# One block turn and two transfers in place of eight score transposes, in a four-layer graph network

## The chip, the cores and the metric

The kernel runs on one core of one Trainium2 chip. The core has five engines: TensorE (PE, matrix products), VectorE (DVE), ScalarE (ACT), GpSimd (POOL) and SyncE (SP), which here only issues transfers (DMA). Each engine works through its own instructions in order, and they meet through semaphores. The metric is the time of one execution in microseconds; less is better.

## The reference

A batch of 32 graphs with 256 nodes and 128 features passes through four graph layers, each with a residual and a layer norm:

```python
x = _layernorm(x + L0(x, adj, adj, ...))   # gated neighbour sums
x = _layernorm(x + L1(x, adj, ...))        # two linear layers with batch norms over all nodes
x = _layernorm(x + L2(x, adj, W, a))       # attention
x = _layernorm(x + L3(x, adj, ...))        # two graph convolutions, then LSTMs over windows of 1 to 4 nodes
```

The change is in the attention, and around it:

```python
Wh = jnp.einsum('bnf,fo->bno', h, W)
s1, s2 = Wh @ a1, Wh @ a2
e = s1[:, :, None] + s2[:, None, :]
e = jnp.where(e >= 0, e, 0.2 * e)
e = jnp.where(adj[None] == 0, -jnp.inf, e)
h_prime = jnp.einsum('bij,bjo->bio', jax.nn.softmax(e, axis=-1), Wh)
```

So each node i has a score s1[i], and the row of all s2[j] of its graph must stand beside it: the second score has to be spread from one value per partition (a node is a partition) to a row of 256 values that every partition holds.

## The kernel before, in words

The batch is cut into 8 groups of 4 graphs; a group is 8 tiles of 128 nodes x 128 features (two tiles a graph). The layers L0 and L1 come first for all groups, since the batch norms need every node. Then the groups go through attention (A), the graph convolutions of L3 (B), the LSTMs (L) and the last norm (T) in a pipeline of slots: slot s = 2 to 9 holds A of group s, B of group s - 1, L of group s - 2 and T of group s - 3, as far as these groups exist. Groups 0 and 1 have their attention ahead of the slots. A is in the slots 2 to 7, T from slot 3 on; slot 8 has B, L and T, slot 9 has only L and T and cuts its LSTM into two lanes so that one computes while the other waits. The order of every engine's work in a slot is written out by hand in one function `slot` per engine (L491 for SyncE, L631 GpSimd, L1026 TensorE, L1372 ScalarE, L1974 VectorE), so what stands behind what is read there.

The LSTMs are eleven steps k = 0 to 10 (windows of 1, 1, 2, 2, 3, 3, 3, 4, 4, 4, 4 nodes). A step is: x(k), TensorE's product of the inputs (L958); h(k), its product of the last state (L984), for all but the first step of a window; the gates on ScalarE (L1334); the cell on VectorE (`lstm_cell`, L1846; the first step of a window needs only this line); the tanh of the cell on ScalarE (L1370); the state on VectorE (`lstm_state`, L1874). In the code `inner(k)` is the cell, `state(k)` the state, `cell(k)` both. h(k) waits for the state of step k - 1, and so does the x(k) that begins the windows of another length: x(4) waits for state 3, x(7) for state 6. Where a step is done in halves, L1892 to L1904 and L1871 stand for the cell and the first half of the state.

Around the change in a slot with A:

- VectorE: statistics of the first norm (L1721, L1549 to L1559); `t_blocks` (L1945), which turns 32 x 32 blocks of a finished LSTM group for its way back to node order; the cell and state of step 2; `a_dots` (L1728), sixteen products-and-sums of the residual tiles with two vectors, which give both scores before scaling; `a_s12` (L1734), scores times rstd; the cell and state of step 3; `a_max` (L1745), eight times: row of scores plus mask, and its maximum; the cell and state of step 4.
- GpSimd: rstd of the first norm (L526), OFF = mean x rstd (L532), then `scaled(s + 2)` (L586), the batch norm's scale on a group that comes two slots later, which returns at once for s = 6 and 7; later the copies of `carry_residual` (L604) and `carry_blocks` (L614), which wait for turns by VectorE.
- ScalarE: gates and tanh of step 2, `a_spread` (L1304), eight `norm_apply` (L1169), the gates of step 3.
- TensorE: x(3), h(3), `a_rows` (L854), `a_weigh0` (L923), x(4), x(5), h(5), x(6), `a_weigh1` (L932), h(6), `a_spread1` (L941), x(7), x(8) and so on. `a_rows` takes column t of S12, repeated 128 times, and transposes it with the identity: that gives one 128-column piece of the row of scores, on all partitions, in PSUM (PA).
- SyncE: `weave` (L484) stores the turned blocks to DRAM, waits for the store, and loads them back in another order in four transfers; `t_sum` (L1952) on VectorE waits for those. Behind it in the queue stand `move_residual`, `move_blocks` and the store of the output.

Slot 8 ends B: `a_hidden` (L1834) on VectorE takes the relu of `a_spread1`'s whole result into HT, the LSTM's input. In slot 9 `t_blocks` stands between step 0 and step 1; the products of lane 1 for step 2 (L1006, PA) wait for state 1.

Of the kernel before, what the change touches and what calls it, by code (L numbers as in the profile page):

```python
# [20 lines left out]
F32 = mybir.dt.float32  # L21
# [79 lines left out]
def build(nc, x, xt, adj, early_in, later_in, lstm_w, out):  # L101
    ctx = ExitStack()
    with ctx:
# [164 lines left out]
        def before(g):  # L268
# [25 lines left out]
        ln = [{s: sem(f"ln{k}_{s}") for s in ("stats", "sum", "dif", "sqd", "mean", "m2", "var", "rstd", "off", "out")} for k in range(4)]  # L294
# [4 lines left out]
        (yt_ok, y_ps, z1_ok, x2t_ps, x2t_ok, s2_ps, wh_ps, wh_ok, max_ok, eb_a, eb_ok, lin_ok, exps_ok,  # L299
         et_ps, pt_ok, att_ps, rd_ok, z2_ok, sp_ps, sp_ok, y0_ps, y0_ok, h0_ok, y1_ps,  # L300
         y1_ok, h1_ps, h1_ok, ht_ok, zf_ok) = (sem(n) for n in (
             "yt_ok", "y_ps", "z1_ok", "x2t_ps", "x2t_ok", "s2_ps", "wh_ps", "wh_ok", "max_ok", "eb_a",
# [114 lines left out]
        BLOCKS = late[:, 2, COLS:2 * COLS]  # L417

# [25 lines left out]
        def _(sp):  # L444
# [219 lines left out]
        def _(pe):  # L664
# [165 lines left out]
            def a_scores(g, h):  # L830
                pe.wait_ge(x2t_ok, halves(g, h))
                f = front(g)
                pe.matmul(f.PB[:, h * BANK:(h + 1) * BANK], WA2[:], f.X2T[:, h * BANK:(h + 1) * BANK],
                          start=True, stop=True).then_inc(s2_ps, 1)
# [191 lines left out]
            def slot(s, par, A, B, L, T):  # L1026
# [55 lines left out]
                a_rows(s) if A else None  # L1082
# [79 lines left out]
        def _(act):  # L1162
# [115 lines left out]
            def a_lin(g, some):  # L1278
                f = front(g)
                for b in some:  # L1280
                    act.wait_ge(wh_ok, 2 * g + b // 2 + 1) if g < 2 else act.wait_ge(s12_ok, g - 1)
# [90 lines left out]
            def slot(s, par, A, B, L, T):  # L1372
# [104 lines left out]
        def _(dve):  # L1477
# [245 lines left out]
            def a_dots(g):  # L1723
                dve.wait_ge(z1_ok, 2 * (g - 1))
                dve.wait_ge(rows_ok, 1)
                for k, junk in enumerate((one_a, one_c)):
                    for t in range(TILES):
                        dve.tensor_tensor_reduce(nth(junk, t), nth(Z, t), WAR[:, k], 1.0, 0.0,  # L1728
                                                 ALU.mult, ALU.add, DOT[:, k, t:t + 1]).then_inc(dots_ok, 1)

            def a_s12(g):
                dve.wait_ge(dots_ok, 2 * TILES * (g - 1))
                dve.wait_ge(ln[1]["rstd"], 2 * (g + 1))
                dve.tensor_tensor(S12[:], DOT[:], RSD[0][:].unsqueeze(1).broadcast_to([P, 2, TILES]), ALU.mult).then_inc(s12_ok, 1)  # L1734

            def a_max(g, h=None):

                dve.wait_ge(s2_ps, halves(g, h))
# [8 lines left out]

            def a_bias(g, h=None):

                ts = tls(h)  # L1750
                dve.wait_ge(wh_ok, halves(g, h)) if g < 2 else dve.wait_ge(s12_ok, g - 1)
# [190 lines left out]
            def t_blocks(g, par):  # L1942
                dve.wait_ge(h_ok, NSTEP * (g + 1))
                for c in range(NC):
# [29 lines left out]
            def slot(s, par, A, B, L, T):  # L1974
# [65 lines left out]
                a_hidden(s - 1, 1 - par) if B and not A else None  # L2040
# [114 lines left out]
```

## Time and profile before

| | |
|---|---|
| median of 3 runs | 616.72 us (616.62 to 617.77) |
| the profiled execution | 617.1 us, span of its instructions 615.3 us |
| TensorE busy | 596.5 us, 97% of the span, 2560 products |
| VectorE busy | 495.3 us, 80% |
| ScalarE busy | 431.7 us, 70% |
| GpSimd busy | 242.3 us, 39% |
| granted TensorE clock | 0.997 of full speed, mean over the span |
| chain that ended last | TensorE 62%, VectorE 10%, ScalarE 8% of the span |

A timeline row gives the start and the length of a group of instructions in us, its engine, its source line (L854 is line 854), the operation, the tiles (out<-in), shapes, and in brackets how long the engine stood idle before it and which instruction ended that. Instructions of one engine overlap a little, so the time that one costs is the distance to the next start. TensorE's products are pipelined and their ends are modelled: one row may seem to reach some 0.17 us into the next. The groups of the page merge all instructions of one line and shape.

### The profile page before, as it was taken

What the parts mean: (1) busy time and instruction counts of PE and PEld (TensorE: products, weight loads), DVE (VectorE), ACT (ScalarE), POOL (GpSimd) and SP (SyncE); (2) the same over time, 40 slices, a digit from 0 to 9 for tenths busy, and PEclk for the clock granted to TensorE, in tenths of its full rate; (3) what the DMA queues carried; (4) which work ended last, traced back from release to release, by engine and by line L of the source; (5) the groups of instructions that cost most, each with busy time, mean ns of one, the idle gap of its engine ahead of it and who ended that gap; (6) DMA issues with size and microseconds to landing.
All of it is one profiled execution on the core that took longest, in us unless ns stands there. A gap on an engine that the chain in (4) does not pass through costs nothing.

```text
span 615.3 us, 9582 instructions
## 1 busy us (share of the span) xinstructions
PE 596.5 (97%) x2560; PEld 416.8 (68%) x2560; DVE 495.3 (80%) x1673; ACT 431.7 (70%) x1000; POOL 242.3 (39%) x384
## 2 busy tenths in 40 slices
PE   8999999999999999999999999999999999999994
PEld 6645556447886687678658767865876686675894
DVE  3999999876857778889888988888898878466576
ACT  3678877965947776785778668567867867556774
POOL 1465461005134074238607733860673075003013
PEclk9999999999999999999999999999999999999998
DMA  8434000000000010201111110111112011100201
GB/s 320 158 137 172 0 3 0 0 1 1 2 2 1 0 42 3 69 14 40 60 35 36 44 68 10 35 63 42 31 47 70 1 35 69 35 0 34 70 2 69
DMA packets 14982, 28.00 MB, mean 46 GB/s; under 512 B 2896, under 2 KB 10192, under 8 KB 14800
## 3 DMA queue, kind: packets, MB, share of 16 engines
q1 hardware_dynamic: 14928, 27.40, 12.9%
q8 instruction: 20, 0.33, 0.2%
q14 instruction: 34, 0.28, 0.1%
HBM read 15.72 MB, written 7.86 MB: 38 GB/s over the span
## 4 chain that ended last, share of the span: by engine, by line
PE 62%; DVE 10%; ACT 8%; issue 4%; POOL 1%; DVEq 0%; POOLq 0%; ACTq 0%
PE QQ L958 19%; PE QQ L984 13%; PE PA L941 4%; PE PB L932 2%; ACT X L1169 2%; PE PA L914 2%; PE PB L792 2%; PE PA L792 2%; PE PB L894 2%; PE PA L894 2%; DVE HB L1745 1%; ACT raw L1334 1%; PE QQ L973 1%; PE QQ L1006 1%; PE PA L745 1%
## 5 line engine op out<-in xcount | busy, mean ns | idle before, releaser
L1334 ACT ACTIVATE raw<-QQ,BL 128x256 f32<-128x256 f32 (+2 forms) x279 | 149.3, 558 | 67.1 <-PE QQ L984 29.4
L958 PE MATMUL QQ<-HT,WT 128*128 128x512 f32 (+2 forms) x516 | 163.7, 464 | 0.1
L958 PEld LDWEIGHTS QQ<-HT,WT 128*128 128x128 f32 x516 | 96.1, 190 | 53.3 <-issue 26.8
L526 POOL TENSOR_TENSOR RSD<-VAR,pw 128x4 f32<-128x4 f32 (+1 forms) x43 | 59.4, 1381 | 153.9 <-DVE VAR L1559 153.9
L984 PE MATMUL QQ<-HB,WT 128*128 128x256 f32 (+2 forms) x336 | 100.8, 443 | 1.6 <-DVE HB L1874 1.4
L984 PEld LDWEIGHTS QQ<-HB,WT 128*128 128x128 f32 x336 | 61.1, 190 | 32.6 <-issue 13.4
L604 POOL COPY HB<-HB 32x256 f32<-32x256 f32 x60 | 27.4, 456 | 96.5 <-DVE HB L1696 93.1
L1370 ACT ACTIVATE raw<-raw 128x256 f32<-128x256 f32 (+4 forms) x79 | 37.2, 471 | 29.7 <-DVE raw L1856 19.8
L614 POOL COPY HB<-HB 32x256 f32<-32x256 f32 x96 | 40.8, 425 | 33.0 <-DVE HB L1767 26.9
L1846 DVE SCALAR_TENSOR_TENSOR raw<-raw 128x256 f32<-128x256 f32 (+2 forms) x60 | 32.1, 535 | 9.6 <-ACT raw L1334 8.7
L594 POOL TENSOR_SCALAR X<-four,MEAN,RSD 128x128 f32<-128x128 f32 x64 | 37.4, 596 | 1.6
L1169 ACT ACTIVATE X<-Z,OFF,RSD 128x128 f32<-128x128 f32 x80 | 31.8, 482 | 2.5 <-POOL OFF L532 2.5
L1874 DVE SCALAR_TENSOR_TENSOR HB<-raw 128x256 f32<-128x256 f32 (+4 forms) x42 | 22.0, 525 | 13.5 <-ACT raw L1370 13.5
L1297 ACT ACTIVATE HB<-HB,EB 128x256 f32<-128x256 f32 x64 | 30.8, 499 | 0.2
L745 PE MATMUL PA<-AHT,X 128*128 128x256 f32 x128 | 29.6, 384 | 1.3 <-ACT X L1169 1.3
L628 POOL TENSOR_SCALAR four<-HB,MEAN,RSD 128x128 f32<-128x128 f32 x56 | 30.0, 549 | 0.7
L914 PE MATMUL PA<-AD,X 128*128 128x256 f32 x128 | 30.2, 379 | 0.0
L759 PE MATMUL QQ<-one_b,later 128*128 128x512 f32 x64 | 29.1, 597 | 0.6 <-ACT one_b L1203 0.6
L941 PE MATMUL PA<-AD,Y 128*128 128x256 f32 x128 | 29.2, 380 | 0.0
L914 PEld LDWEIGHTS PA<-AD,X 128*128 128x128 f32 x128 | 24.2, 190 | 7.1 <-issue 4.1
L745 PEld LDWEIGHTS PA<-AHT,X 128*128 128x128 f32 x128 | 23.7, 190 | 7.7 <-issue 4.8
L941 PEld LDWEIGHTS PA<-AD,Y 128*128 128x128 f32 x128 | 24.2, 190 | 4.3
(260 smaller groups left out, 1213.9 us busy)
## 6 DMA issues: line engine op xcount, KB each, us to landing
four<-in_x SPq DMA_DIRECT2D x8, 512.0 KB, 4.1
raw<-in_xt SPq DMA_DIRECT2D x8, 512.0 KB, 7.1
HB<-HB SPq DMA_DIRECT2D x116, 32.0 KB, 1.8
woven<-HB SPq DMA_DIRECT2D x7, 512.0 KB, 2.6
HB<-woven SPq DMA_DIRECT2D x28, 128.0 KB, 2.8
out<-four SPq DMA_DIRECT2D x7, 512.0 KB, 2.7
WT<-in_lstm SPq DMA_DIRECT2D x1, 2048.0 KB, 8.0
later<-in_later SPq DMA_DIRECT2D x1, 725.5 KB, 10.5
```

Of the source, the lines that this page charges most:

```text
L526: pool.tensor_tensor(RSD[kk][:, ts], VAR[kk][:, ts], pw[:, ts], ALU.pow).then_inc(ln[k]["rstd"], some)
L594: pool.tensor_scalar(tile_of(X1, g, c, b), nth(f.Z2, t), MEAN[f.kk2][:, t:t + 1], RSD[f.kk2][:, t:t + 1], ALU.add, ALU.mult).then_inc(ln[2 ...
L614: pool.tensor_copy(block_at(1, h, c, q), block_at(0, h, q, c)).then_inc(carried_ok, 1)
L745: mm = pe.matmul(PA[:, b * NODES:(b + 1) * NODES], tile_of(X1, g, m, b), AHT[:, m, :], start=(m == 0), stop=(m == NC - 1))
L914: mm = pe.matmul(PA[:, b * NODES:(b + 1) * NODES], tile_of(X1, g, m, b), ADJT[:, m, :], start=(m == 0), stop=(m == NC - 1))
L941: mm = pe.matmul(PA[:, b * NODES:(b + 1) * NODES], turned(Y, m, b), ADJT[:, m, :], start=(m == 0), stop=(m == NC - 1))
L958: mm = pe.matmul(steps_view(Q[q], k), WT[:, 0, (p - 1) * 4 + q, :], ht_view(par, k), start=True, stop=(s == 0))
L984: pe.matmul(Q[q][:, 0:nw * GB], WT[:, 1, (p - 1) * 4 + q, :], HS[:, (k - 1) % 2, 0:nw * GB], start=False, stop=True).then_inc(g_ps, 1)
L1169: act.activation(nth(to, t), nth(z, t), ACT.Identity, bias=OFF[kk][:, t:t + 1], scale=RSD[kk][:, t:t + 1]).then_inc(ln[k]["out"], 1)
L1334: act.activation(TG[q][:, at:n], Q[q][:, at:n], ACT.Tanh, scale=0.5 if q == G else 0.25, bias=BL[:, p - 1, q:q + 1]).then_inc(g_ok, 1)
L1370: act.activation(TC[:, at:n], CELL[:, at:n], ACT.Tanh, scale=0.5).then_inc(tc_ok, 1)
L1846: dve.scalar_tensor_tensor(out=target[:, 0:n], in0=TG[I][:, 0:n], scalar=1.0, in1=TG[G][:, 0:n], op0=ALU.add, op1=ALU.mult).then_inc(cell_ ...
```

## The change

In the slots 2 to 7 `a_rows` goes. VectorE makes the second score first: its eight dots, then times rstd (`a_score(s, 1)`), then `a_turn_scores`, one 32 x 32 block turn of the eight scores each repeated 32 times, which leaves each 32-partition block with its own 256 scores in a row. SyncE stores one row of each block to DRAM (`scores`, 4 KB), waits for it, and loads all 1024 scores to every partition (`ROWS`, 512 KB), at the head of the slot's queue. `a_max` becomes `a_max_some` and reads ROWS in SBUF instead of PA in PSUM; six of its tiles stand ahead of the cell of step 4 and two behind it. The dots of the first score stand between and behind the cell and the state of step 2, and `t_blocks` behind them. A part of `t_sum` moves from ahead of state 4 to behind the cell and the state of step 5. `a_spread1` no longer waits for the maxima.

In slot 8 `a_spread1` is cut in two halves, behind x(8) and behind x(9), and the relu of `a_hidden` goes from VectorE to ScalarE, also in halves. In slot 9 `t_blocks` goes from behind step 0 to behind step 1, its second half behind the first cell of lane 1.

```diff
@@ SyncE
+            def spread_scores(g):
+                sp.wait_ge(s2_ok, halves(g, None))
+                sp.wait_ge(ln[2]["out"], TILES * 2) if g == 2 else None
+                sp.dma_start(scores[g].rearrange("(t q i) -> q t i", q=4, i=32),
+                             BYROW[0:P:32].rearrange("q (t i) -> q t i", i=32)).then_inc(scores_in, 16)
+                sp.wait_ge(scores_in, 32 * (g - 2) + 16)
+                sp.dma_start(ROWS, scores[g].unsqueeze(0).broadcast_to([P, TILES * P])).then_inc(scores_in, 16)
             for s in range(2, GROUPS + 2):
+                spread_scores(s) if s < GROUPS else None
                 weave(s - 3) if s >= 3 else None
@@ TensorE
-            def a_rows(g):
-                pe.wait_ge(s12_ok, g - 1)
-                reach(pe, sp_ok, 2 * g)
-                for b in range(GB):
-                    for c in range(NC):
-                        t = 2 * b + c
-                        mm = pe.transpose(turned(PA, c, b), S12[:, 1, t:t + 1].broadcast_to([P, P]), ident[:])
-                mm.then_inc(s2_ps, 2)
...
-                pe.wait_ge(max_ok, upto(g + 2) * TILES) if g else None
...
-                    a_spread1(LAST)
-                    for k in range(7, NSTEP):
-                        x(k)
-                        h(k) if STEPS[k][1] else None
+                    x(7)
+                    x(8)
+                    a_spread1(LAST, 0)
+                    h(8)
+                    x(9)
+                    a_spread1(LAST, 1)
+                    h(9)
+                    x(10)
+                    h(10)
...
-                a_rows(s) if A else None
@@ ScalarE
-                a_mixed(s, (0, 1)) if A else None
+                a_mixed(s, (0, 1)) if A else a_hidden(LAST, 1 - par, 0) if B else None
                 gates(9)
                 state(9)
-                a_mixed(s, (2, 3)) if A else None
+                a_mixed(s, (2, 3)) if A else a_hidden(LAST, 1 - par, 1) if B else None
@@ VectorE
+            def a_score(g, k):
+                dve.wait_ge(dots_ok, 2 * TILES * (g - 2) + (2 - k) * TILES)
+                dve.wait_ge(ln[1]["rstd"], 2 * (g + 1))
+                dve.tensor_tensor(S12[:, k], DOT[:, k], RSD[0][:], ALU.mult).then_inc(s12_ok, 1)
+            def a_turn_scores(g):
+                dve.wait_ge(s12_ok, 2 * (g - 2) + 1)
+                dve.transpose(BYROW.rearrange("p (t i) -> p t i", i=32),
+                              S12[:, 1].unsqueeze(2).broadcast_to([P, TILES, 32])).then_inc(s2_ok, 2)
+            def a_max_some(g, a, b):
+                dve.wait_ge(scores_in, 32 * (g - 1))
+                for t in range(a, b):
+                    dve.tensor_tensor_reduce(MS[:, t], ROWS[:, t // 2 * NODES:(t // 2 + 1) * NODES], NEG[:, t % 2], 1.0, -3e38,
+                                             ALU.add, ALU.max, MX[0][:, t:t + 1]).then_inc(max_ok, 1)
...
                 if s == LAST + 2:
                     cell(0)
-                    t_blocks(s - 3, 1 - par)
                     cell(1)
+                    t_blocks(s - 3, 1 - par, 0)
                     for k in range(LANED, NSTEP):
                         for l in range(2):
                             lane_cell(k, l)
+                            t_blocks(s - 3, 1 - par, 1) if (k, l) == (LANED, 1) else None
...
                     norm_small(1, 0, s)
-                t_blocks(s - 3, 1 - par) if T else None
-                cell(2)
                 if A:
-                    a_dots(s)
-                    a_s12(s)
+                    a_dots(s, 1, 0, TILES)
+                    a_score(s, 1)
+                    a_turn_scores(s)
+                inner(2)
+                a_dots(s, 0, 0, 4) if A else None
+                state(2)
+                if A:
+                    a_dots(s, 0, 4, TILES)
+                    a_score(s, 0)
+                t_blocks(s - 3, 1 - par, 0, 1) if T else None
                 cell(3)
-                a_max(s) if A else None
+                a_max_some(s, 0, 6) if A else None
                 inner(4)
-                t_sum(s - 3, (0,)) if T else None
+                a_max_some(s, 6, TILES) if A else None
                 state(4)
                 a_biased0(s - 1) if B else None
                 a_bias(s) if A else None
                 t_sum(s - 3, (1,)) if T else None
                 inner(5)
-                t_sum(s - 3, (2, 3)) if T else None
+                t_sum(s - 3, (0, 2)) if T else None
                 state(5)
+                t_sum(s - 3, (3,)) if T else None
...
-                a_hidden(s - 1, 1 - par) if B and not A else None
```

## Rows read from the trace of the kernel before

**Rows 1.** TensorE's timeline, s = 5: start, us, engine, line, operation, tiles, shapes, count.

```profile
365.86 1.04 PE L854 MATMUL PA<-ident,S 128*128 128x128 f32 x8
366.73 1.88 PE L923 MATMUL PB<-one_b,later 128*128 128x512 f32 x4
368.45 4.24 PE L958 MATMUL QQ<-HT,WT 128*128 128x340 f32 x14
372.74 2.55 PE L984 MATMUL QQ<-HB,WT 128*128 128x340 f32 x8
```

**Rows 2.** VectorE's timeline, s = 5; bracketed: idle time before, its end.

```profile
356.85 2.11 DVE L1945 STREAM_TRANSPOSE HB<-HT 128x512 f32<-128x512 f32 x2
358.87 0.66 DVE L1846 SCALAR_TENSOR_TENSOR raw<-raw 128x512 f32<-128x512 f32 x1
360.29 1.01 DVE L1874 SCALAR_TENSOR_TENSOR HB<-raw 128x512 f32<-128x512 f32 x1 [0.77 <-ACT raw L1370]
...
367.95 0.42 DVE L1874 SCALAR_TENSOR_TENSOR HT<-raw 128x256 f32<-128x256 f32 x1
368.28 0.42 DVE L1745 CUSTOM_DVE_ANT_0 HB<-PA,NEG 128x256 f32<-128x256 f32 x1
...
371.04 0.51 DVE L1846 SCALAR_TENSOR_TENSOR raw<-raw 128x340 f32<-128x340 f32 x1
...
372.17 0.51 DVE L1874 SCALAR_TENSOR_TENSOR HB<-raw 128x340 f32<-128x340 f32 x1 [0.29 <-ACT raw L1370]
```

**Rows 3.** ScalarE's timeline, s = 5.

```profile
359.56 0.63 ACT L1370 ACTIVATE raw<-raw 128x512 f32<-128x512 f32 x1 [1.12 <-DVE raw L1846]
...
364.08 1.24 ACT L1334 ACTIVATE raw<-QQ,BL 128x512 f32<-128x512 f32 x2
```

**Rows 4.** VectorE's groups of instructions, whole span: busy us, mean ns, idle before.

```profile
L1728 DVE CUSTOM_DVE_ANT_0 one_c<-Z,WAR 128x128 f32<-128x128 f32 x48 | 10.6, 282 | 0.0
```

**Rows 5.** GpSimd's timeline, s = 5.

```profile
351.96 1.49 POOL L526 TENSOR_TENSOR RSD<-VAR,pw 128x4 f32<-128x4 f32 x1 [2.04 <-DVE VAR L1559]
...
357.09 1.64 POOL L526 TENSOR_TENSOR RSD<-VAR,pw 128x8 f32<-128x8 f32 x1 [1.25 <-DVE VAR L1559]
358.89 0.70 POOL L532 TENSOR_TENSOR OFF<-MEAN,RSD 128x8 f32<-128x8 f32 x1 [0.17 <-POOL RSD L526]
359.58 1.19 POOL L586 TENSOR_SCALAR HB<-HB,BN 128x1024 f32<-128x1024 f32 x1
```

**Rows 6.** GpSimd's timeline, s = 2.

```profile
195.53 0.20 POOL L532 TENSOR_TENSOR OFF<-MEAN,RSD 128x8 f32<-128x8 f32 x1 [0.17 <-POOL RSD L526]
195.71 1.20 POOL L586 TENSOR_SCALAR HB<-HB,BN 128x1024 f32<-128x1024 f32 x1
```

**Rows 7.** VectorE's timeline, s = 2.

```profile
196.00 1.44 DVE L1874 SCALAR_TENSOR_TENSOR HB<-raw 128x512 f32<-128x512 f32 x1 [0.77 <-ACT raw L1370]
```

**Rows 8.** DMA issues of the page: count, KB each, us from issue to landing.

```profile
woven<-HB SPq DMA_DIRECT2D x7, 512.0 KB, 2.6
```

**Rows 9.** TensorE's timeline, s = 8 and 9.

```profile
544.79 3.62 PE L941 MATMUL PA<-AD,Y 128*128 128x256 f32 x16
548.24 3.19 PE L958 MATMUL QQ<-HT,WT 128*128 128x256 f32 x14
552.04 1.99 PE L984 MATMUL QQ<-HB,WT 128*128 128x256 f32 x8 [0.61 <-DVE HB L1874]
...
556.27 1.99 PE L984 MATMUL QQ<-HB,WT 128*128 128x256 f32 x8 [0.51 <-DVE HB L1874]
...
570.40 0.70 PE L1006 MATMUL PA<-HT,WT 128*128 128x256 f32 x2 [1.55 <-DVE HT L1874]
```

**Rows 10.** VectorE's timeline, s = 8 and 9.

```profile
546.48 0.33 DVE L1874 SCALAR_TENSOR_TENSOR HT<-raw 128x172 f32<-128x172 f32 x1
...
568.60 0.71 DVE L1888 SCALAR_TENSOR_TENSOR raw<-raw 128x256 f32<-128x256 f32 x2
```

**Rows 11.** ScalarE's timeline, s = 9.

```profile
566.02 2.06 ACT L1334 ACTIVATE raw<-QQ,BL 128x512 f32<-128x512 f32 x3
```

More of the change, by code:

```diff
@@ L293, in build @@
         rows_ok, dots_ok, s12_ok, px_ps, px_ok = (sem(n) for n in ("rows_ok", "dots_ok", "s12_ok", "px_ps", "px_ok"))
-        ln = [{s: sem(f"ln{k}_{s}") for s in ("stats", "sum", "dif", "sqd", "mean", "m2", "var", "rstd", "off", "out")} for k in range(4)]
+        ln = [{s: sem(f"ln{k}_{s}") for s in ("stats", "sum", "dif", "sqd", "mean", "m2", "var", "rstd", "off", "out") if (k, s) != (2, "off")}
+              for k in range(4)]
+        scores_in = sem("scores_in")
         agg1_ps, agg1_ok, hid_ps, hid_ok, hid_st = (
@@ L298, in build @@
         act_ok, out2_ps, out2_ok, out2_st = (sem(n) for n in ("act_ok", "out2_ps", "out2_ok", "out2_st"))
-        (yt_ok, y_ps, z1_ok, x2t_ps, x2t_ok, s2_ps, wh_ps, wh_ok, max_ok, eb_a, eb_ok, lin_ok, exps_ok,
+        (yt_ok, y_ps, z1_ok, x2t_ps, x2t_ok, s2_ok, wh_ps, wh_ok, max_ok, eb_a, eb_ok, lin_ok, exps_ok,
          et_ps, pt_ok, att_ps, rd_ok, z2_ok, sp_ps, sp_ok, y0_ps, y0_ok, h0_ok, y1_ps,
          y1_ok, h1_ps, h1_ok, ht_ok, zf_ok) = (sem(n) for n in (
-             "yt_ok", "y_ps", "z1_ok", "x2t_ps", "x2t_ok", "s2_ps", "wh_ps", "wh_ok", "max_ok", "eb_a",
+             "yt_ok", "y_ps", "z1_ok", "x2t_ps", "x2t_ok", "s2_ok", "wh_ps", "wh_ok", "max_ok", "eb_a",
              "eb_ok", "lin_ok", "exps_ok", "et_ps", "pt_ok", "att_ps", "rd_ok", "z2_ok", "sp_ps",
@@ L417, in build @@
         BLOCKS = late[:, 2, COLS:2 * COLS]
+        scores = nc.dram_tensor("scores", (GROUPS, TILES * P), F32, kind="Internal").ap()
+        BYROW = late[:, 2, 0:NODES]
+        ROWS = four[:, 1]
         def stored(g):
@@ L833, in a_scores @@
                 pe.matmul(f.PB[:, h * BANK:(h + 1) * BANK], WA2[:], f.X2T[:, h * BANK:(h + 1) * BANK],
-                          start=True, stop=True).then_inc(s2_ps, 1)
+                          start=True, stop=True).then_inc(s2_ok, 1)
             def a_project(g, h):
@@ L1280, in a_lin @@
                 for b in some:
-                    act.wait_ge(wh_ok, 2 * g + b // 2 + 1) if g < 2 else act.wait_ge(s12_ok, g - 1)
+                    act.wait_ge(wh_ok, 2 * g + b // 2 + 1) if g < 2 else act.wait_ge(s12_ok, 2 * (g - 1))
                     act.wait_ge(max_ok, TILES * g + 2 * b + 2)
@@ L1312, in a_state, with a_hidden @@
                 act.wait_ge(h1_ps, halves(0, h))
+                act.activation(by_batch(HT[:, par])[:, 2 * h:2 * h + 2], PA[:, part(h)].rearrange("p (b n) -> p b n", n=NODES),
+                               ACT.Relu, scale=2.0).then_inc(h1_ok, 1)
+            def a_hidden(g, par, h):
+                act.wait_ge(h1_ps, halves(g, h))
+                reach(act, ht_ok, 2 * (g - 1))
                 act.activation(by_batch(HT[:, par])[:, 2 * h:2 * h + 2], PA[:, part(h)].rearrange("p (b n) -> p b n", n=NODES),
@@ L1721, in a_norm1_some, with a_dots @@
                     dve.bn_stats(STL[0][:, t, :], nth(Z, t)).then_inc(ln[1]["stats"], 1)
-            def a_dots(g):
+            def a_dots(g, k, a, b):
                 dve.wait_ge(z1_ok, 2 * (g - 1))
                 dve.wait_ge(rows_ok, 1)
[L1726 to L1732, printed above, removed]
-                dve.wait_ge(ln[1]["rstd"], 2 * (g + 1))
-                dve.tensor_tensor(S12[:], DOT[:], RSD[0][:].unsqueeze(1).broadcast_to([P, 2, TILES]), ALU.mult).then_inc(s12_ok, 1)
+                for t in range(a, b):
+                    dve.tensor_tensor_reduce(nth((one_a, one_c)[k], t), nth(Z, t), WAR[:, k], 1.0, 0.0,
+                                             ALU.mult, ALU.add, DOT[:, k, t:t + 1]).then_inc(dots_ok, 1)
+            def a_score(g, k):
+                dve.wait_ge(dots_ok, 2 * TILES * (g - 2) + (2 - k) * TILES)
+                dve.wait_ge(ln[1]["rstd"], 2 * (g + 1))
+                dve.tensor_tensor(S12[:, k], DOT[:, k], RSD[0][:], ALU.mult).then_inc(s12_ok, 1)
[3 more added lines that the diff above has]
+                              S12[:, 1].unsqueeze(2).broadcast_to([P, TILES, 32])).then_inc(s2_ok, 2)
             def a_max(g, h=None):
-                dve.wait_ge(s2_ps, halves(g, h))
+                dve.wait_ge(s2_ok, halves(g, h))
                 reach(dve, att_ps, GB * before(g))
@@ L1746, in a_max @@
                                                  ALU.add, ALU.max, f.MX[:, t:t + 1]).then_inc(max_ok, 1)
+            def a_max_some(g, a, b):
+                dve.wait_ge(scores_in, 32 * (g - 1))
+                for t in range(a, b):
+                    dve.tensor_tensor_reduce(MS[:, t], ROWS[:, t // 2 * NODES:(t // 2 + 1) * NODES], NEG[:, t % 2], 1.0, -3e38,
+                                             ALU.add, ALU.max, MX[0][:, t:t + 1]).then_inc(max_ok, 1)
             def a_bias(g, h=None):
                 ts = tls(h)
-                dve.wait_ge(wh_ok, halves(g, h)) if g < 2 else dve.wait_ge(s12_ok, g - 1)
+                dve.wait_ge(wh_ok, halves(g, h)) if g < 2 else dve.wait_ge(s12_ok, 2 * (g - 1))
                 dve.wait_ge(max_ok, TILES * g + ts.stop)
@@ L1940, in lane_state, with t_blocks @@
                                          in1=steps_view(TC, k)[:, a:b], op0=ALU.add, op1=ALU.mult).then_inc(v.h, 1)
-            def t_blocks(g, par):
+            def t_blocks(g, par, *some):
                 dve.wait_ge(h_ok, NSTEP * (g + 1))
-                for c in range(NC):
+                for c in some:
                     dve.transpose(BLOCKS.rearrange("p (r c b i) -> p c b r i", r=4, c=NC, b=GB)[:, c],
```

## The prediction

> **What bounds the kernel now.** I read the page first, then TensorE's timeline over one full slot, then the chain of waits over the same slot, and last VectorE, ScalarE and GpSimd side by side in its front half. Slot s = 5 stands for s = 2 to 7, whose rows repeat.
>
> TensorE issues back to back. In [rows 1] each group starts where the one before it ended, counted by columns: the eight transposes of `a_rows` fill 365.86 to 366.73 (0.87 us), `a_weigh0` fills 366.73 to 368.45, then come x(4) and x(5) (14 instructions), then h(5) at 372.74. So TensorE work that goes away seems to pay in full. It doesn't have to: x(4) may start only when VectorE has written the state of step 3, and that ends at 367.95 + 0.42 = 368.37 [rows 2]. The chain of waits says the same: in the front half of a slot it runs on VectorE and ScalarE, and from h(5) to the slot's end on TensorE alone. The front half is a tie, within 0.1 us at x(4) and some 0.2 us at h(5). Whatever leaves TensorE there leaves a hole unless state 3 comes earlier.
>
> What sets state 3 is one line of work. VectorE: two block turns (L1945) from 356.85, then the cell of step 2 (L1846) at 358.87 [rows 2]. ScalarE waits for that cell (1.12 us idle), takes its tanh at 359.56, then works without a pause through `a_spread` and eight `norm_apply` to the gates of step 3 at 364.08 [rows 3]; from there to state 3 it is 368.37 - 364.08 = 4.3 us. A delay of the cell of step 2 goes one to one into state 3, and x(4).
>
> **The change in the slots s = 2 to 7.** Ahead of the cell of step 2 the change takes out the block turns, 358.87 - 356.85 = 2.02 us [rows 2], and puts in eight dots, the score times rstd, and the spreading turn. Dots: 10.6 us for 48 in [rows 4], 0.22 each, so 1.77 us: 356.85 to 358.62. The score waits for GpSimd's rstd, which ends at 357.09 + 1.64 = 358.73 [rows 5]. GpSimd can be held up by a dot that it meets: the rstd at 351.96, met by a state update of VectorE, took 1.49 us for a smaller tile. I allow 0.1 us: 358.85. The small product and its hand-over to the turn are estimated at 0.25 us. The turn writes 256 columns per partition; no row shows one from a repeated column. By L1945 (2.02 us for 1024) it is 0.50 us, by the 256-column operations of L1745 ((371.04 - 368.28)/8 = 0.345 us) it is 0.35 us [rows 2]; I take 0.4, both ends stay in the range. So the cell of step 2 could start at 359.5, 0.65 us late.
>
> It then meets GpSimd. In s = 2 to 5 the queue of GpSimd goes on from rstd to OFF (L532) and to `scaled` (L586, 1.19 us on 1024 columns) [rows 5]; in s = 6 and 7 `scaled` returns at once. While L586 runs, a VectorE operation that reads two SBUF tiles stands still: in s = 2, L586 ends at 195.71 + 1.20 = 196.91 [rows 6], and L1874, begun at 196.00, took 1.44 us and ended at 197.44 [rows 7], 0.53 us after L586, whereas an operation of its size takes 0.66 (L1846 in [rows 2]). In s = 5 the same L1874 took 1.01 us beside L586 [rows 2]. In the kernel before it was the cell that came first: L532 took 0.70 us there against 0.20 in s = 2 [rows 5, 6], being held until the cell ended. After the change the order turns over: L532 starts 0.16 us after rstd, takes 0.20, so L586 starts at 359.2, before the cell is ready at 359.5, and ends at 360.4. The cell ends 0.53 us later, at 360.95, where it ended at 358.87 + 0.66 = 359.53. The shift is 1.4 us.
>
> The Trainium skill, page SBUF — State Buffer, section Who interferes with whom, has this as a rule that speaks against the change: a VectorE instruction with two SBUF inputs contends with a GpSimd instruction that reads SBUF, and the one that issues first keeps the port for its whole length. By that rule the sum for these slots is the one made here; without it, it is that of the first rival. The two L1874 agree with it.
>
> State 3 then comes at 368.37 + 1.4 = 369.8, x(4) at 369.85. Without `a_rows` TensorE is ready at 368.45 - 0.87 = 367.58 and stands idle 2.3 us. x(4) and x(5) take 372.74 - 368.45 - 0.2 = 4.1 us, so h(5) starts at 373.95: **+1.2 us a slot** for s = 2 to 5, 4.8 in all. h(5) also needs state 4. Six maxima instead of eight stand ahead of the cell of step 4, from 368.28 + 1.4 to 371.75; state 4 follows as before by 372.17 - 371.04 + 0.51 = 1.64 us, at 373.4 [rows 2]. That is earlier than TensorE needs it, so the two maxima moved behind the cell (0.69 us) gain nothing. In s = 6 and 7 only the 0.65 us counts: x(4) at 369.1, h(5) at 373.2, **+0.45 us** each, 0.9 in all.
>
> Edits at nothing, with their cover. The other eight dots, the second product and the moved block turns (1.77 + 0.25 + 2.02 us) stand on VectorE behind state 2 and end before the gates of step 3 (shifted to 365.5) reach it; if that cover were gone they would add to state 3. State 2 itself comes near 362.5 and h(3) may wait 0.1 to 0.2 us for it, which `a_weigh0` and the idle time absorb. The maxima read SBUF now instead of PSUM: the dots read two SBUF tiles and cost no more per column. GpSimd has nothing to run at that time, since `carry_residual` waits for turns made later. The sums of `t_sum` change places after h(5), where VectorE waits for ScalarE and TensorE.
>
> The transfers: SyncE's queue now holds the score's store, a wait for its landing, and a 512 KB load ahead of `weave`. Behind that wait stand `weave` and, behind it, `move_residual`. The rows land in about 2.6 us for each (the nearest row, 512 KB to `woven` [rows 8]), so ROWS stands near 366 at the latest and the maxima want it at 369.7. The weave starts after the moved block turns (near 365.7), needs two such times, some 371.5, and `t_sum` wants it after 375. Cost taken: 0, at most 2 us a slot if the load were three times slower than that row.
>
> **The last two slots.** In s = 8 `a_spread1` (16 instructions, 548.24 - 544.79 = 3.45 us [rows 9]) no longer covers the wait for state 6, which ends at 546.48 + 0.33 = 546.81 [rows 10]: x(7) starts at 546.9, 2.1 us after TensorE is free. x(7) and x(8) take 14 x 0.2156 = 3.0 us and half of `a_spread1` 1.7: h(8) at 551.6 (before: 552.04). h(8), x(9) and the other half, 24 x 0.2156 = 5.2, put h(9) at 556.8 (before: 556.27 [rows 9]). The two waits are filled, but the new one is larger: **+0.5 us** (0.2 to 0.9). The relu on ScalarE falls into its gaps; if it didn't, x(0) of the next slot would wait for it. In s = 9 TensorE waited 1.55 us at 570.40 for state 1 [rows 9], whose cell stood behind the block turns until 568.60 [rows 10]. With the turns behind state 1 the cell goes when ScalarE has the gates; the tanh can't start before ScalarE ends the third gate at 566.02 + 2.06 = 568.08 [rows 11], against about 569.0 (cell's first half from 568.60): **-1.0 us** (-0.7 to -1.55). The block turns then hide while TensorE works on both lanes.
>
> **Sum.** 4.8 + 0.9 + 0.5 - 1.0 = +5.2 us. The profiled execution took 617.1 us (span 615.3), which is 0.4 above the median 616.72: 622.3 for such an execution, 621.9 for a median.
>
> **The rivals.**
> *The cell gets past GpSimd* (the score is ready sooner than I think, or L586 doesn't hold this cell). Then all six slots cost 0.45 us: 2.7 - 0.5 = +2.2, 618.9. For it: my margin in the race is only 0.3 us. Against it: the two L1874 [rows 2, 7]. With a quick turn and 0.25 us a slot it is +1.0, which can't be told from no change. Chance 0.14 above that line and 0.09 within it.
> *GpSimd's rstd waits for all eight dots.* Each dot reads two SBUF tiles, and the rstd at 351.96 took half a microsecond more beside one such operation [rows 5]. If rstd starts at 358.65 rather than 357.09, the cell shifts by 1.5 us more in all six slots: +9, 631. Against it: there the delay ended with one operation. With transfers that come late (the same sign), chance 0.09.
> *Faster: the path ahead of the cell is shorter after all.* The place is the cell of step 2, and the point from which it decides is 358.87: if it starts no later, x(4) stays at 368.45, the moved maxima count, h(5) gains 0.2 us in six slots, and with 1.55 us in s = 9 and nothing lost in s = 8 it is -2.8, 613.9. Against it: rstd ends at 358.73 and three steps follow it. Chance 0.05.
> *The change does not relieve TensorE at all* (transposes gone, hole in their place) is part of my forecast, not beside it.
>
> **How the numbers follow.** Forecast 621.9 with chance 0.63: its own range runs from 619.5 (turn 0.35, slot 9 at its best) to 624.5 (turn 0.5, rstd held 0.2 us, 1.5 us a slot). With the first rival the range reaches down to 617.9; a little of the third up to 625.5. A measurement of this kernel can tell some 0.2%, 1.2 us, from no change. Faster 0.05, within 0.2% 0.09, slower 0.86.
>
> **What would show it.** Right: in s = 2 to 5 L1846 of step 2 takes some 1.3 us or more and ends 0.5 us after L586; x(4) starts over 1 us after `a_weigh0` has run out, with TensorE idle before it; in s = 6 and 7 that idle time is smaller by 0.7 us; TensorE is idle 2 us before x(7) of s = 8, and less than 1 us at state 1 of s = 9. Wrong: L1846 starts before L586 in these slots, or x(4) follows `a_weigh0` at once, or the maxima wait for the load of the scores.

## The result, and the profile after

The changed kernel takes 626.9 us in the median (625.4 to 628.5) beside 616.8 us: a ratio of 1.016, 95% interval 1.0144 to 1.0175. The forecast was 621.9 us (617.9 to 625.5): the sign was right, the loss twice as large. The profiled execution, the slowest of the four, took 628.5 us; its span is 626.5 us against 615.3, and its mean granted clock 0.986 against 0.997. In the new file lines move: L1846 is now L1872, L1874 is L1900, L1370 is L1386, L586 is L601, L958 is L963, L984 is L989, L923 is L929, L941 is L946; L1753 is the new turn. In the experiments' files they can lie a few lines further on.

VectorE in s = 5, where [rows 2] showed the cell of step 2 at 358.87 with 0.66 us (start us, us, engine, line, operation, tiles, shapes):

```profile
365.43 0.45 DVE L1753 STREAM_TRANSPOSE HB<-S 128x256 f32<-128x256 f32 x1
365.80 1.34 DVE L1872 SCALAR_TENSOR_TENSOR raw<-raw 128x512 f32<-128x512 f32 x1
...
375.57 0.42 DVE L1900 SCALAR_TENSOR_TENSOR HT<-raw 128x256 f32<-128x256 f32 x1
375.90 0.42 DVE L1771 CUSTOM_DVE_ANT_0 HB<-four,NEG 128x256 f32<-128x256 f32 x1
```

GpSimd and ScalarE in the same slot, against [rows 5] and [rows 3]:

```profile
363.42 1.64 POOL L541 TENSOR_TENSOR RSD<-VAR,pw 128x8 f32<-128x8 f32 x1 [1.25 <-DVE VAR L1575]
365.22 0.20 POOL L547 TENSOR_TENSOR OFF<-MEAN,RSD 128x8 f32<-128x8 f32 x1 [0.17 <-POOL RSD L541]
365.41 1.20 POOL L601 TENSOR_SCALAR HB<-HB,BN 128x1024 f32<-128x1024 f32 x1
```

```profile
367.18 0.63 ACT L1386 ACTIVATE raw<-raw 128x512 f32<-128x512 f32 x1 [2.40 <-DVE raw L1872]
```

The scale of GpSimd starts at 365.41, ahead of the cell, and ends at 366.61; the cell takes 1.34 us and ends at 367.14, 0.53 us later. In s = 7, where the scale isn't there, the same cell behind the same turn takes 0.65 us:

```profile
478.01 0.65 DVE L1872 SCALAR_TENSOR_TENSOR raw<-raw 128x512 f32<-128x512 f32 x1
```

The rest of the line follows: ScalarE idles 2.40 us where it idled 1.12, state 3 is written from 375.57 on, and the maxima (L1771) follow at once: they do not wait for the transfers (nor in the other five slots), whose issues SyncE's timeline shows at 365.90 and 367.61:

```profile
365.90 0.57 SPq L500 DMA_DIRECT2D scores<-HB  x1
367.61 0.34 SPq L503 DMA_DIRECT2D four<-scores  x1
```

TensorE, x(4) and x(5) of s = 2, 3 and 4 (206.17, 263.37, 320.55), h(5) of s = 4 (324.66), then s = 5, against [rows 1]:

```profile
206.17 5.96 PE L963 MATMUL QQ<-HT,WT 128*128 128x340 f32 x14 [1.96 <-DVE HT L1900]
...
263.37 5.96 PE L963 MATMUL QQ<-HT,WT 128*128 128x340 f32 x14 [1.97 <-DVE HT L1900]
...
320.55 4.27 PE L963 MATMUL QQ<-HT,WT 128*128 128x340 f32 x14 [1.96 <-DVE HT L1900]
324.66 2.45 PE L989 MATMUL QQ<-HB,WT 128*128 128x340 f32 x8
...
372.19 1.88 PE L929 MATMUL PB<-one_b,later 128*128 128x512 f32 x4
376.04 5.96 PE L963 MATMUL QQ<-HT,WT 128*128 128x340 f32 x14 [1.97 <-DVE HT L1900]
381.84 2.45 PE L989 MATMUL QQ<-HB,WT 128*128 128x340 f32 x8
```

One idle time, then the stretches behind those of s = 5, 4 and 8 (window in us, its length, time in which TensorE was busy with the number of its instructions, granted clock, share of the DMA engines, GB/s):

```profile
374.10:376.00 1.90, 0.00 (x0) 1.00 0.26 74
376.04:381.80 5.76, 5.76 (x14) 0.70 0.21 66
320.60:324.50 3.90, 3.90 (x14) 1.00 0.38 106
556.65:561.60 4.95, 4.95 (x15) 0.66 0.01 3
```

Here lies what the forecast left out. `a_weigh0` starts at 372.19 and, by [rows 1], fills 1.72 us; x(4) starts at 376.04, so TensorE is idle 2.13 us, as forecast (2.3). But then the same fourteen products of x(4) and x(5) take 5.80 us (376.04 to 381.84) in s = 5 and 4.11 us (320.55 to 324.66) in s = 4. In s = 5 the granted clock of that stretch is 0.70, for part of it the lower of the two levels (1.2 GHz); in s = 4 it is 1.00. That costs 1.7 us each time. Call such a fall of the clock a drop. In this execution there are four, behind the idle times of s = 2, 3, 5 and 8: four times 1.7 us, or 6.8 us.

From one h(5) to the next the kernel before needs 54.50 us, from its h(5) of s = 4 (the row stops at the end of its window; only its start is read),

```profile
318.24 1.98 PE L984 MATMUL QQ<-HB,WT 128*128 128x340 f32 x6
```

to 372.74 [rows 1]. After, s = 4 to s = 5 takes 381.84 - 324.66 = 57.18, 2.68 more; s = 3 to s = 4, without the drop, takes 55.50 (269.16 to 324.66), 0.97 more than before (263.71 to 318.24).

In s = 6 and 7 the scale isn't there and the idle time is shorter; the clock stays, and the group takes 4.27 us where it took 5.96:

```profile
432.77 4.27 PE L963 MATMUL QQ<-HT,WT 128*128 128x340 f32 x14 [1.52 <-DVE HT L1900]
...
487.56 4.27 PE L963 MATMUL QQ<-HT,WT 128*128 128x340 f32 x14 [1.27 <-DVE HT L1900]
```

The last two slots, against [rows 9]:

```profile
556.65 4.98 PE L963 MATMUL QQ<-HT,WT 128*128 128x256 f32 x14 [1.91 <-DVE HT L1900]
561.46 1.89 PE L946 MATMUL PA<-AD,Y 128*128 128x256 f32 x8
...
581.70 0.70 PE L1011 MATMUL PA<-HT,WT 128*128 128x256 f32 x2 [0.47 <-DVE HT L1900]
```

x(7) waits 1.91 us for state 6, and x(7) and x(8) take 4.81 us where 3.0 were counted, at a granted clock of 0.66. State 1 of s = 9 is waited for 0.47 us instead of 1.55.

### The profile page after: what moved, and what is told of

It is laid out like the page before. It is cut to its first block, busy times and chain, and to the rows that moved or that the text cites. A ratio compares the mean times of both kernels' runs of the same rounds, so it can differ in the third digit from the quotient of the medians.

```text
span 626.5 us, 9518 instructions
## 1 busy us (share of the span) xinstructions
PE 597.4 (95%) x2512; PEld 416.0 (66%) x2512; DVE 498.4 (80%) x1684; ACT 432.5 (69%) x1002; POOL 241.0 (38%) x384
## 4 chain that ended last, share of the span: by engine, by line
PE 60%; ACT 10%; DVE 9%; issue 4%; POOL 2%; DVEq 0%; ACTq 0%; POOLq 0%
PE QQ L963 23%; PE QQ L989 11%; PE PA L946 4%; ACT X L1178 3%; PE PB L938 2%; ACT raw L1350 2%; PE PB L807 2%; PE PA L807 2%; POOL RSD L541 2%; PE PB L900 2%; PE PA L900 2%; PE PA L760 1%; DVE HT L1900 1%; PE PA L920 1%; DVE raw L1872 1%
## 5 line engine op out<-in xcount | busy, mean ns | idle before, releaser
L963 PE MATMUL QQ<-HT,WT 128*128 128x512 f32 (+2 forms) x516 | 170.7, 480 | 12.7 <-DVE HT L1900 12.6
L963 PEld LDWEIGHTS QQ<-HT,WT 128*128 128x128 f32 x516 | 99.7, 197 | 70.3 <-issue 30.9
L989 PE MATMUL QQ<-HB,WT 128*128 128x256 f32 (+2 forms) x336 | 100.0, 440 | 0.6 <-DVE HB L1900 0.6
L989 PEld LDWEIGHTS QQ<-HB,WT 128*128 128x128 f32 x336 | 61.5, 190 | 29.4 <-issue 11.2
L1386 ACT ACTIVATE raw<-raw 128x256 f32<-128x256 f32 (+4 forms) x79 | 37.1, 470 | 34.0 <-DVE raw L1882 20.1
L1872 DVE SCALAR_TENSOR_TENSOR raw<-raw 128x256 f32<-128x256 f32 (+2 forms) x60 | 34.4, 574 | 13.7 <-ACT raw L1350 13.1
L946 PE MATMUL PA<-AD,Y 128*128 128x256 f32 x128 | 29.4, 380 | 0.0
L946 PEld LDWEIGHTS PA<-AD,Y 128*128 128x128 f32 x128 | 24.3, 191 | 4.2
L1900 DVE SCALAR_TENSOR_TENSOR HB<-raw 128x256 f32<-128x256 f32 (+4 forms) x42 | 20.3, 483 | 8.0 <-ACT raw L1386 8.0
```

The costliest lines, as they stand in the source:

```text
L963: mm = pe.matmul(steps_view(Q[q], k), WT[:, 0, (p - 1) * 4 + q, :], ht_view(par, k), start=True, stop=(s == 0))
L989: pe.matmul(Q[q][:, 0:nw * GB], WT[:, 1, (p - 1) * 4 + q, :], HS[:, (k - 1) % 2, 0:nw * GB], start=False, stop=True).then_inc(g_ps, 1)
L1386: act.activation(TC[:, at:n], CELL[:, at:n], ACT.Tanh, scale=0.5).then_inc(tc_ok, 1)
L1872: dve.scalar_tensor_tensor(out=target[:, 0:n], in0=TG[I][:, 0:n], scalar=1.0, in1=TG[G][:, 0:n], op0=ALU.add, op1=ALU.mult).then_inc(cell_ ...
```

## The experiments

Two theories stood after the result. A: the order on VectorE and GpSimd makes the idle times, which cost the forecast's +5 us, and the granted clock behind them costs the other 5. B: the clock is a by-catch, and something else (the transfers, a second wait) costs the difference. Each time is a median, compared with the kernel before on the same chip (617.4 us for the first four, 617.0 us for the others).

**e1_warm: the changed kernel with TensorE's idle time filled.** The products that fill it are read by nobody.

```diff
                     h(6)
+                    spin(PA[:, 0:P], 9)
                     x(7)
...
                 a_weigh0(s - 1) if B else None
+                spin(PA[:, 0:P], 9) if A and s < 6 else None
                 x(4)
```

> The changed kernel with nine dummy products (18 instructions of 128 columns, 1.94 us, into a PSUM tile that nobody reads) in the hole before x(4) in s = 2 to 5 and before x(7) in s = 8; state 3 and state 6 come no earlier. Theory A (an idle TensorE of about 2 us is followed by 3.4 us at the lower granted clock, 1.7 us lost each time): no drop is left, four drops times 1.7 us come back, 626.9 - 6.8 = 620 us, mean granted clock as in the kernel before (0.997). Rival B (the slow products behind x(4) come from the 512 KB load of the scores or from something else in the change, and the rest of the surprise lies elsewhere): 626.5 to 627.5 us and the slow stretches stay.

Measured: 622.3 us (621.9 to 622.5), ratio 1.008 (1.0064 to 1.0095), granted clock 0.998. TensorE's timeline and the stretch of x(4) and x(5), s = 5:

```profile
370.63 2.17 PE L683 MATMUL PA<-ones 128*128 128x128 f32 x18
372.76 4.27 PE L963 MATMUL QQ<-HT,WT 128*128 128x340 f32 x14
376.87 2.45 PE L989 MATMUL QQ<-HB,WT 128*128 128x340 f32 x8
```

```profile
372.70:376.90 4.20, 4.20 (x16) 1.00 0.32 96
```

x(4) is as late as before, since it waits for the same state, yet its group takes 4.11 us again (376.87 - 372.76). For 45 products that nobody needs (90 instructions) the loss falls from 626.9 - 616.8 = 10.1 us to 622.3 - 617.4 = 4.9, which is nearly the sum of the forecast (+5.2). A holds; the clock is half of the loss. The expected 620 us took four drops off the median, but four belong to the profiled execution: between the two profiled executions the difference is 628.5 - 621.9 = 6.6 us, the 6.8 of four drops.

**e2_port: the changed kernel, GpSimd's scale held back until the cell of step 2 is done.**

```diff
                     rstd(1, 0, s)
+                    pool.wait_ge(cell_ok, NSTEP * (s - 2) + 3)
                     scaled(s + 2)
```

> The changed kernel, GpSimd's scaling of a later group waits for the cell of step 2, so that it can't hold the cell. If that hold is what makes the hole before x(4) in s = 2 to 5 longer than in s = 6 and 7: the cell of step 2 takes 0.7 us again, the holes shrink from 2.1 to about 1.5 us, the drops of the clock there go too: 4 x 0.6 + 3 x 1.7 = 7.5, 626.9 - 7.5 = 619.4 us with one drop left, in s = 8. If the hold is not the cause: 627 us.

Measured: 620.1 us (619.2 to 621.7), ratio 1.0048 (1.003 to 1.0066). The cell on VectorE, the scale on GpSimd, x(4) on TensorE, s = 5:

```profile
360.40 0.65 DVE L1873 SCALAR_TENSOR_TENSOR raw<-raw 128x512 f32<-128x512 f32 x1
```

```profile
361.16 1.43 POOL L601 TENSOR_SCALAR HB<-HB,BN 128x1024 f32<-128x1024 f32 x1 [1.13 <-DVE raw L1873]
```

```profile
366.93 1.88 PE L930 MATMUL PB<-one_b,later 128*128 128x512 f32 x4
369.95 4.27 PE L964 MATMUL QQ<-HT,WT 128*128 128x340 f32 x14 [1.14 <-DVE HT L1901]
```

The cell takes 0.65 us instead of 1.34, so the collision is worth 0.69 us, and TensorE's idle time goes from 2.13 to 1.30 us (369.95 - 366.93 - 1.72). Behind 1.30 us the clock does not fall: against the profiled execution of the changed kernel four slots give back the collision (0.69 each) and three drops, 7.9 us by that count, 628.5 - 620.7 = 7.8 measured. The drop in s = 8 is still there, as expected. The Trainium skill's rule (page SBUF — State Buffer, section Who interferes with whom: the instruction that issues first keeps the shared port for its whole length) is borne out by the pair 1.34 and 0.65, and by the held cell ending 0.53 us behind the scale, nearly an undisturbed cell's length.

**e3_s8: the kernel before with the moves of slot 8 alone** (the hunks of the diff for `a_spread1` and `a_hidden`).

```diff
-                    a_spread1(LAST)
-                    for k in range(7, NSTEP):
-                        x(k)
-                        h(k) if STEPS[k][1] else None
+                    x(7)
+                    x(8)
+                    a_spread1(LAST, 0)
+                    h(8)
...
-                a_hidden(s - 1, 1 - par) if B and not A else None
```

> The kernel before with nothing but the change of slot 8 (second graph product in halves behind x(8) and x(9), the relu on ScalarE). Theory A: 2 us idle before x(7), then the lower clock for 3.4 us: +2.6 us, 619.4. My prediction's own price, without the clock: +0.5, 617.3. If the move only fills waits, as its place suggests: -1.4, 615.4.

Measured: 618.3 us, ratio 1.0019 (1.0009 to 1.0029), in ten runs: seven between 617.8 and 618.4, three between 619.5 and 619.6. TensorE in the profiled run, one of the seven:

```profile
547.39 3.29 PE L958 MATMUL QQ<-HT,WT 128*128 128x256 f32 x14 [1.91 <-DVE HT L1886]
550.52 1.89 PE L941 MATMUL PA<-AD,Y 128*128 128x256 f32 x8
```

The idle time is the same 1.91 us as in the changed kernel, but here x(7) and x(8) take 3.13 us, not 4.81. So the same gap is followed by the lower clock in some executions (the traces of the changed kernel and of e2_port) and not in others. The two clusters lie some 1.3 us apart, somewhat less than a drop, and the upper three runs have granted clocks of 0.992 to 0.993 where the seven have 0.995 to 0.998. That the upper three held the drop is inferred from this: only one run was traced. The expected 619.4 is met by those three alone. Without the drop the moves cost some 0.8 us (the seven lie near 618.2), inside the term's 0.2 to 0.9.

**e4_cell_first: the changed kernel, slot 8 as before, and the cell of step 2 ahead of most of the new work.** GpSimd's scale waits for the first score as well.

```diff
+                    pool.wait_ge(s12_ok, 2 * (s - 1))
                     scaled(s + 2)
...
+                a_dots(s, 1, 0, 4) if A else None
+                inner(2)
                 if A:
-                    a_dots(s, 1, 0, TILES)
+                    a_dots(s, 1, 4, TILES)
                     a_score(s, 1)
                     a_turn_scores(s)
-                inner(2)
-                a_dots(s, 0, 0, 4) if A else None
                 state(2)
                 if A:
-                    a_dots(s, 0, 4, TILES)
+                    a_dots(s, 0, 0, TILES)
```

> The changed kernel with slot 8 as before and another order on VectorE: four dots, then the cell of step 2, then the other dots of the second score, the score and its turn, the state, the dots of the first score, the block turns; GpSimd's scaling waits for the first score, so that it falls beside the block turns, which read one tile. If the cell of step 2 is what moved state 3: state 3 comes some 0.3 us earlier than in the kernel before, x(4) idles about 0.5 us instead of 2.1, no drop of the clock, -0.5 us in each of six slots and -1.2 in s = 9: 612.6 us. If the place of the cell doesn't matter (state 3 is late for another reason, such as the scores' transfers): the hole stays at 1.4 us or more and the time above 618.

Measured: 613.8 us (613.2 to 614.1), ratio 0.9941 (0.9927 to 0.9956): faster than both kernels, though 1.2 us above the expected 612.6. TensorE, s = 4 (first line) and s = 5:

```profile
313.40 4.27 PE L964 MATMUL QQ<-HT,WT 128*128 128x340 f32 x14 [0.51 <-DVE HT L1896]
...
365.04 1.88 PE L930 MATMUL PB<-one_b,later 128*128 128x512 f32 x4
367.43 4.27 PE L964 MATMUL QQ<-HT,WT 128*128 128x340 f32 x14 [0.51 <-DVE HT L1896]
```

One slot takes 367.43 - 313.40 = 54.03 us, 0.47 less than before, with dots, turn and both transfers all there. So neither spreading the scores by transfers nor taking the transposes away makes the loss; the place of the new work on VectorE, with the place of GpSimd's scale, does.

**e5_s9: the kernel before with the move of slot 9 alone** (`t_blocks` behind state 1, its second half behind the first cell of lane 1).

```diff
                     cell(0)
-                    t_blocks(s - 3, 1 - par)
                     cell(1)
+                    t_blocks(s - 3, 1 - par, 0)
                     for k in range(LANED, NSTEP):
                         for l in range(2):
                             lane_cell(k, l)
+                            t_blocks(s - 3, 1 - par, 1) if (k, l) == (LANED, 1) else None
```

> The kernel before, with one move of the change alone: in the last round the second transposed block of the previous pair (t_blocks) is split in two, and its second half goes behind the first lane turn of state 1. Theory: the chain of the last round runs over state 1, whose start this move brings 1.0 us forward (the term -1.0 of the prediction's sum; the profile of the changed kernel showed 1.2), and nothing else takes the gain: 616.0 to 616.4 beside a kernel before of 617.2. Rival: the gain seen in the changed kernel came from the new state of that round's queues as a whole, and the move alone gives nothing: 617.2.

Measured: 616.0 us (615.6 to 616.3), ratio 0.9981 (0.9971 to 0.999). VectorE, then TensorE, s = 9:

```profile
568.65 0.42 DVE L1874 SCALAR_TENSOR_TENSOR HT<-raw 128x256 f32<-128x256 f32 x1
568.99 1.08 DVE L1945 STREAM_TRANSPOSE HB<-HT 128x512 f32<-128x512 f32 x1
```

```profile
569.13 0.70 PE L1006 MATMUL PA<-HT,WT 128*128 128x256 f32 x2 [0.47 <-DVE HT L1874]
```

The turn now follows state 1, and TensorE waits 0.47 us instead of 1.55: -1.1 us, as the term -1.0 said.

**e7_refill: e4 with products in place of the eight transposes**, nobody reads them.

```diff
                 a_weigh0(s - 1) if B else None
+                spin(PA[:, 0:P], 4) if A else None
                 x(4)
```

> The kernel of e4_cell_first with four dummy products (eight instructions, 0.87 us) put ahead of x(4) in the rounds s=2 to 7, in the place and of the length of the eight transposes that the change removed; nothing reads them. It asks what the removal of the transposes is worth by itself. Theory: with the cell of step 2 early, x(4) waits 0.67 us for state 3 in every round, so of 0.87 us refilled only 0.2 a round shows: 6 x 0.2 = 1.2 us over e4, 613.8 + 1.2 = 615.0. Rival: the removed transposes are what e4 gains (its six rounds gained 0.4 each), so refilling them gives back the full 0.87 a round: 613.8 + 5.2 = 619.0.

Measured: 614.2 us (613.9 to 614.6), ratio 0.995 (0.9936 to 0.9965) against 0.9941 for e4. TensorE, s = 5:

```profile
364.88 1.88 PE L930 MATMUL PB<-one_b,later 128*128 128x512 f32 x4
366.59 1.05 PE L684 MATMUL PA<-ones 128*128 128x128 f32 x8
367.48 4.17 PE L964 MATMUL QQ<-HT,WT 128*128 128x340 f32 x14
```

The two intervals overlap, so the times don't tell the refill from nothing; the traces do: one slot takes 54.12 us (x(4) to x(4), 313.36 to 367.48) against 54.03 in e4, some 0.1 us a slot for 0.89 us refilled. That is the theory, with half of its 1.2 us, and the rival (+5.2) is out. The transposes stood in time that TensorE would have waited anyway. What e4 gains comes with its order on VectorE, which brings state 3 and state 4 in time; which of its moved lines gives most of the 0.47 us was not tried.

**e8_delay: the kernel before, eight dots more ahead of the cell of step 2**, nothing else (their sums are overwritten later).

```diff
+            def a_idle(g):
+                dve.wait_ge(z1_ok, 2 * (g - 1))
+                for t in range(8):
+                    dve.tensor_tensor_reduce(nth(one_a, t), nth(Z, t), WAR[:, 0], 1.0, 0.0,
+                                             ALU.mult, ALU.add, DOT[:, 0, t:t + 1])
...
                 t_blocks(s - 3, 1 - par) if T else None
+                a_idle(s) if A else None
                 cell(2)
```

> The kernel before with nothing of the change but a delay: eight dummy dots on VectorE (1.77 us, by the 0.22 us that one of the change's dots takes) ahead of the cell of step 2 in the rounds s=2 to 7; scores, transposes and transfers as before. Theory: what the change costs in these rounds is the late cell alone, so a delay of its dots' length does the same without a transfer: state 3 comes 1.4 to 1.8 us later, x(4) is 1.0 to 1.7 us late a round, 6 to 10 us in all, and more where the idle time is followed by a lower granted clock: 623 to 634. Rival: VectorE has slack ahead of that cell and what costs time in the changed kernel is the spread by transfers or the missing products: below 619.

Measured: 627.4 us (626.9 to 628.2), ratio 1.0163 (1.0146 to 1.018): as much as the whole change loses, from a delay alone, at a granted clock of 0.998. That the two totals agree is chance: here there is no drop, and all of it is waiting, while in the changed kernel waiting is half. VectorE (the dot that meets GpSimd's scale, then the cell) and TensorE (h(3), x(4)), s = 5:

```profile
364.44 1.12 DVE L1734 CUSTOM_DVE_ANT_0 one_a<-Z,WAR 128x128 f32<-128x128 f32 x1
...
366.12 0.68 DVE L1852 SCALAR_TENSOR_TENSOR raw<-raw 128x512 f32<-128x512 f32 x1
```

```profile
368.32 3.70 PE L984 MATMUL QQ<-HB,WT 128*128 128x512 f32 x8 [1.00 <-DVE HB L1880]
...
375.91 4.27 PE L958 MATMUL QQ<-HT,WT 128*128 128x340 f32 x14 [1.18 <-DVE HT L1880]
```

The dots take 2.5 us here (363.61 to 366.12), more than the 1.77 counted, because one is held by the scale and takes 1.12 us. The cell is late by that much, and TensorE's waits, 1.00 us at h(3) and 1.18 us at x(4), add up to nearly it. From h(5) to h(5) the slots s = 3 to 5 cost 2.5 to 2.8 us more each, s = 6 and 7, where no scale meets the dots, 1.9 and 1.7, and s = 2, where no block turns stand ahead of the cell, nothing: with the turns there is no slack ahead of that cell. The dots here stand ahead of state 2 as well, so the delay falls into two gaps, and behind neither of them does the clock fall. The expectation was right in the total, but it had all of the delay at x(4), while h(3) took nearly half.

**e9_relu: e4 with the relu of slot 8 on ScalarE**, in halves, but the spread kept ahead of x(7).

```diff
-                    a_spread1(LAST)
+                    a_spread1(LAST, 0)
+                    a_spread1(LAST, 1)
...
-                a_mixed(s, (0, 1)) if A else None
+                a_mixed(s, (0, 1)) if A else a_hidden(LAST, 1 - par, 0) if B else None
...
-                a_hidden(s - 1, 1 - par) if B and not A else None
```

> The kernel of e4_cell_first with one further piece of the change for slot 8: ScalarE takes the last hidden activation (relu) in two halves behind its earlier work, and VectorE leaves it out, while the spread of the first score still stands ahead of x(7) on TensorE as in the kernel before. Theory: slot 8 of the changed kernel is slower only by the idle time before x(7), which this form does not make, and the wait of h(8) for the activation (0.77 us) goes: 613.8 - 0.7 = 613.1. Rival: the activation on ScalarE delays its work for state 3 of that slot, and x(7) is late as in the changed kernel: 614.5 to 616.

Measured: 612.4 us (612.1 to 613.1), ratio 0.9923 (0.9908 to 0.9937), the best of all. TensorE, s = 8:

```profile
545.24 3.19 PE L964 MATMUL QQ<-HT,WT 128*128 128x256 f32 x14
548.26 1.89 PE L990 MATMUL QQ<-HB,WT 128*128 128x256 f32 x8
```

h(8) follows x(8) at once, where it waited 0.61 us in [rows 9]. The move of the relu was good; what made slot 8 slower was taking the cover from x(7). By the traces slot 8 gains 0.8 us on e4. The two profiled executions differ by 1.7 us, and 0.6 of it lies ahead of the slots, where the two kernels are equal, so it isn't the edit's.

## Why the forecast was right, and where it failed

- **The tie at x(4)** was read rightly. Without the transposes TensorE is free earlier and stands idle, 2.13 us against 2.3. e8_delay shows the other half: a delay ahead of the cell of step 2 goes into TensorE's waits nearly one to one.
- **The collision with GpSimd** came as described. Against [rows 2, 5], the cell ended 1.28 us later after the start of rstd (367.14 - 363.42 = 3.72 against 359.53 - 357.09 = 2.44), counted as 1.4: 0.69 from the scale (e2_port) and some 0.6 from the new order (counted as 0.65). The turn from a repeated column cost 365.80 - 365.43 = 0.37 us, counted as 0.4.
- **+1.2 us a slot in s = 2 to 5** is the term that failed, and with it the forecast. Its step "x(4) and x(5) take 372.74 - 368.45 - 0.2 = 4.1 us" took the pace from a stretch in which TensorE had not stopped. Behind an idle time of 2.1 us the group took 5.80 us in three of these four slots, and the slot cost 2.7 to 2.9, not 1.2. In s = 4, where the clock stayed, it cost 0.97; in e1_warm 0.9 to 1.2.
- **+0.5 us in s = 8** has the same fault: the wait of 2.1 us was seen, and "x(7) and x(8) take 14 x 0.2156 = 3.0 us" was 4.81. Without the drop the slot costs some 0.8 (e1_warm, e3_s8).
- **+0.45 us in s = 6 and 7** came as 0.53 and 0.26 us; their gaps are 1.68 and 1.44 us.
- **-1.0 us in s = 9** came as -1.1 in e5_s9.
- **The edits at nothing** cost nothing: the maxima start without a wait, and e4 gains with both transfers in place. The reason given for the maxima was misread: a dot's 0.22 us for 128 columns is more per column than a maximum's 0.345 us for 256. The maxima from SBUF still follow each other at 0.34 to 0.35 us, as they did from PSUM.
- **The range** held no case for the clock. The sum by measured terms without drops, 4 x 0.97 + 0.53 + 0.26 + 0.8 - 1.1 = +4.4 us, lies near the forecast's +5.2, in part by luck: the slots s = 2 to 5 were counted too dear and s = 8 too cheap. Four drops of 1.7 us add 6.8 and give 11.2, which is the difference of the two spans.

In the kernel before no price of a drop could be read. Its clock is 1.00 in every stretch until TensorE's last product, also ahead of those shown here; only the end of the span, where TensorE has nothing left to do, makes the mean 0.997:

```profile
350.00:611.00 261.00, 253.78 (x1124) 1.00 0.12 38
611.00:616.00 5.00, 0.00 (x0) 0.60 0.28 105
```

TensorE's longest wait there in the slots, 1.55 us in [rows 9], has the clock up behind it and says nothing on the longer gaps that the forecast itself made: they called for a case of their own in the range.

None of the rivals happened. The cell did not get past GpSimd, rstd was not held (1.64 us in both), the cell did not start early.

What is open: why the clock falls behind a gap of 2.1 us in one slot and not in the next (s = 3 and s = 4 have the same gap to 0.01 us), and so how many drops an execution gets. The spread of the changed kernel's runs, 625.4 to 628.5 at clocks of 0.991 to 0.986, fits two to four of them.

## What to carry to other kernels

Taking work from the busiest engine pays only if what it waits for next comes earlier; ask which line of work ends last at that point and put new instructions behind its links, not ahead of them. A hole that a change opens in TensorE's stream has two prices: its length, and the granted clock of the products behind it; look for the second in the profile of a kernel that already has such holes, or keep a case for it in the range. Where VectorE and GpSimd meet in SBUF, look at which of two short instructions goes first: here one wait on GpSimd gave back 0.69 us in each of four slots, and with the drops that went too, the kernel came from 626.9 to 620.1 us.

## What the runs showed of the hardware

- TensorE's granted clock fell to the lower level after idle times of 2.07 to 2.13 us in most cases but not in all (in the changed kernel four of five; in e2_port's slot 8 yes, in e3_s8's traced run no). After idle times of 0.67 to 1.72 us it fell in none of the traced slots. Each drop cost 1.7 us, nearly as much as the gap.
- Products whose result nobody reads, in such a gap, halved the loss (e1_warm: ratio 1.008 against 1.016).
- One VectorE dot, 0.28 us elsewhere, took 1.12 us when GpSimd's scale was running (e8_delay): this small instruction was held as the large cell was. The block turns, which read one tile, took 2.14 us beside the scale (e4_cell_first) against 2.11 where the scale had not begun [rows 2].
